# A router's 0/1 rows made by one comparison a token tile, and a transpose moved ahead of a score group

## Chip, cores and metric

One NeuronCore of a Trainium2 chip runs the whole program. The metric is device time in microseconds (us), the median of several runs. Engines are PE (matmul), DVE (vector), ACT (scalar), POOL (GpSimd), SP (issues DMAs).

## What is computed

Two transformer layers on 2048 tokens of width 512, each with a modulated layer norm, an attention and a feed-forward part.

```
x = x + ga * attn0(norm(x) * (1+ca) + sa)      # windows of 64, hop 32
x = x + gb * moe(norm(x) * (1+cb) + sb)        # 64 experts, 8 chosen per token
x = x + ga * attn1(norm(x) * (1+ca) + sa)      # window 128 and 16 first keys
x = x + gb * ffn(norm(x) * (1+cb) + sb)        # Hadamard, 512 -> 2048 -> 512
```

In `moe` each token goes to eight experts:

```
top_val, top_idx = lax.top_k(probs, 8)
mapping = jnp.where(replace, best_primary, jnp.arange(E))   # some experts merged into others
y = ragged_dot(silu(gate) * up, down)                       # rows sorted by expert
out = zeros.at[tok].add(y * w)
```

## The kernel before

The program is a row of blocks with a barrier of all engines between them: set-up, first attention with the router's scores, routing, experts, second attention, feed-forward. Inside a block every engine has a fixed program, and semaphores order them.

**Routing** turns the chosen experts into a table `slot_rows`: sorted by expert, the 16384 (token, expert) pairs fill up to SLOTS = 192 slot tiles of 128 places. A pair has a slot tile `part[:, 0]` (0 to 191) and a place in it `part[:, 1]` (0 to 127). The table with one token number a place is a sum of outer products on PE: for each of NT = 16 token tiles of 128 tokens, and each of TOPK = 8 choices j, a matmul (L995) of `hot_b` (128 tokens x 128 places, the token's number where the place is this pair's, else 0) by `hot_a` (128 tokens x 192 slot tiles, 1 or 0). All 128 add into bank 1. `hot_a` and `hot_b` are fp16, double buffered (GROUPS = 2): tile t waits until the matmuls of tile t - 2 are done (`table_mm`).

Each row of `hot_a` is one DVE instruction (L1083), so is each of `hot_b` for j below BY_DVE = 5 (L1085). For the other three ACT makes `|place - iota|` (L904) and then `relu(token - token * that)` (L907). PE waits for DVE (`hot_done`) and ACT (`hot_act`). Between the tables' matmuls PE does other work of the block: a Hadamard product of `wd` (L920, for token tiles 0 to 11) and a quarter of a modulation product (L928) a tile. ACT copies their results out (L883, L888, L890) in the same loop. Before the loop PE does two whole modulation products and two small transposes (L988), and DVE works out `part`. POOL has no work in this block. The block ends when DVE has written `slot_rows` (L1091) and ACT has copied the last modulation product.

**The second attention** works in turns written out by hand. In a turn tile s has its scores made, the tile before it, a, has its probabilities transposed and multiplied by the values, w gets the output projection, and y, p, f are later tiles being normalised and projected. PE's order in the last part of a turn is: the output projection of w (L1703), the transposes of a's fourth group of probabilities (`turn_probs(a, 3)`, L1645), the scores of s's fourth group (`scores(s, 3)`, L1635), two transposes of a's probabilities of the first 16 keys (L1715) and one of its inverted row sums (L1717, which raises `pM_mm`), the transposes of f's keys (L1724), and then the products that need what ACT copied: L1730 spreads the inverted row sums and waits for `pM_out`, raised by ACT's copies L1606 and L1607; L1733 and L1737 follow. ACT's order is the two copies of the fourth group (L1579), L1606, L1607, the copy of f's keys (L1617), the exponentials of s's fourth group (L1571). DVE's row maxima of s's fourth group (L1773) follow its scores and are DVE's last work of a turn.

Of the kernel before, what the change touches and what calls it, by code (L numbers as in the profile page):

```python
# [5 lines left out]
ALU = mybir.AluOpType  # L6
ACT = mybir.ActivationFunctionType
# [3 lines left out]
I32 = mybir.dt.int32  # L11
U32 = mybir.dt.uint32
F16 = mybir.dt.float16

P = 128
S, C = 2048, 512
NT = S // P
# [12 lines left out]
E = 64  # L30
TOPK, SELK = 8, 4
# [4 lines left out]
SLOTS = PAIRS // P + E  # L36
# [19 lines left out]
AHEAD = 3  # L56
# [54 lines left out]
def adaln_two_layers(nc, a, out):  # L111
    ctx = ExitStack()
    with ctx:
# [33 lines left out]
        route = sb("route", [P, 8 * C])  # L147
# [3 lines left out]
        slot_iota = sb("slot_iota", [P, SLOTS], F16)  # L151
# [645 lines left out]
        with ExitStack() as ph, nc.Block() as block:  # L797
# [2 lines left out]
            GROUPS = 2  # L800
            up_at, down_at = (lambda r: r * UPW), (lambda r: RING * UPW + r * DOWNW)
            cv = Carver(up_at(AHEAD))
            hot_a = cv(GROUPS * TOPK * SLOTS // 2).bitcast(F16).rearrange("p (b j n) -> p b j n", b=GROUPS, j=TOPK)
            assert cv.at <= RING * UPW
            cv = Carver(down_at(AHEAD))
            hot_b = cv(GROUPS * TOPK * P // 2).bitcast(F16).rearrange("p (b j n) -> p b j n", b=GROUPS, j=TOPK)
            assert cv.at <= KEPT
            cv = Carver(SCRATCH0)
            secT = cv(NT // 2 * P // 2).bitcast(BF16).rearrange("p (i n) -> p i n", n=P)
# [15 lines left out]
            slot_f = cv(NT, TOPK)  # L825
            slot_i = cv(NT, TOPK).bitcast(I32)
            part_i = cv(2, NT, TOPK).bitcast(I32)
            part = cv(2, NT, TOPK)
            minus, tok_minus = cv(NT, TOPK), cv(NT)
            BY_DVE = 5  # L830
            away = masked.rearrange("p t e -> p (t e)")[:, 0:GROUPS * (TOPK - BY_DVE) * P].rearrange("p (b j n) -> p b j n", b=GROUPS, n=P)
            cols, act_c = cv(KC), cv(KC)
            act_b = cv(KC, P)
            spare = cv(1)
# [4 lines left out]
                ("c_in", "rows_in", "ahead_in", "c_done", "c_wide", "cnt_mm", "secT_mm", "secT_out", "moves_done",  # L839
                 "chosen_mm", "chosen_done", "tot_mm", "rank_mm", "eid_done", "eid_mm", "hot_done", "table_mm",  # L840
                 "had_mm", "had_out", "mod_mm", "mod_out", "dve_steps"))
            parts_done, away_done, hot_act = (psem("r_" + n) for n in ("parts_done", "away_done", "hot_act"))
            wT_mm, wT_out, moves_wide, w_mm, w_out, w_stored = (
                psem("r_" + n) for n in ("wT_mm", "wT_out", "moves_wide", "w_mm", "w_out", "w_stored"))
            wm_in = [psem(f"r_wm_in{j}") for j in range(WMB)]
# [4 lines left out]
            @block.sync  # L850
            def _(sp):
                sp.dma_start(cols, a["c_cols"][:, 1]).then_inc(c_in, 16)
                for e in range(AHEAD):
                    sp.dma_start(arena[:, up_at(e):up_at(e) + UPW], a["moe_up"][e].rearrange("p k n -> p (k n)")).then_inc(ahead_in, 16)
                    sp.dma_start(arena[0:FH, down_at(e):down_at(e) + DOWNW], a["moe_down"][e].rearrange("p k n -> p (k n)")).then_inc(ahead_in, 16)
                w = a["L1_wmod"].rearrange("(k p) (j n) -> j p k n", p=P, j=6)
                sp.dma_start(routed.su_row, a["L1_ffn_SU_ug"].partition_broadcast(P)).then_inc(rows_in, 16)
                sp.dma_start(routed.down_row, a["L1_ffn_Wscale_dp"].partition_broadcast(P)).then_inc(rows_in, 16)
                sp.wait_ge(w_out, 2)
                sp.dma_start(h_moe[0:S, C:].rearrange("(t p) e -> p t e", p=P), routed.second.rearrange("p i (t e) -> p (i t) e", e=E)).then_inc(w_stored, 16)  # L860
                for j in range(WMB, 6):
                    sp.wait_ge(mod_mm, j - WMB + 1)
                    sp.dma_start(routed.wm[:, j - WMB], w[j]).then_inc(wm_in[j - WMB], 16)
                sp.wait_ge(w_stored, 16)
                sp.wait_ge(ahead_in, 32 * AHEAD)
                sp.wait_ge(rows_in, 32)

            @block.scalar
            def _(act):
                for n in range(2):  # L870
                    act.wait_ge(secT_mm, n + 1)
                    nc.scalar.copy(secT[:, 4 * n:4 * n + 4].rearrange("p i n -> p (i n)"), psum[6 + n][:]).then_inc(secT_out, 1)
                for n in range(2):
                    act.wait_ge(wT_mm, n + 1)
                    nc.scalar.copy(routed.secondT[:, 4 * n:4 * n + 4].rearrange("p i n -> p (i n)"), psum[2 + n][:]).then_inc(wT_out, 1)
                act.wait_ge(c_in, 16)
                nc.scalar.activation(act_c, cols, ACT.Silu).then_inc(c_done, 1)
                act.wait_ge(c_done, 1)
                nc.scalar.copy(act_b[:], act_c.unsqueeze(2).to_broadcast([P, KC, P])).then_inc(c_wide, 1)

                def had_copy(f):
                    act.wait_ge(had_mm, f + 1)
                    nc.scalar.copy(wd[:, f], had_bank(f)[:]).then_inc(had_out, 1)  # L883

                def mod_copy(j):
                    act.wait_ge(mod_mm, j + 1)
                    if j in (1, 4):
                        nc.scalar.add(mod[:, 1, j], mod_bank(j)[:], 1.0).then_inc(mod_out, 1)  # L888
                    else:
                        nc.scalar.copy(mod[:, 1, j], mod_bank(j)[:]).then_inc(mod_out, 1)  # L890
                for f in range(HAD0):
                    had_copy(f)
                for n in range(2):
                    act.wait_ge(w_mm, n + 1)
                    nc.scalar.copy(routed.second[:, 4 * n:4 * n + 4].rearrange("p i n -> p (i n)"), psum[6 + n][:]).then_inc(w_out, 1)
                mod_copy(0)
                mod_copy(1)
                act.wait_ge(parts_done, 1)
                for t in range(NT):
                    if t >= GROUPS:  # L900
                        act.wait_ge(table_mm, t - GROUPS + 1)
                        act.wait_ge(hot_act, t - GROUPS + 1)
                    for j in range(BY_DVE, TOPK):
                        nc.scalar.activation(away[:, t % GROUPS, j - BY_DVE], slot_iota[:, 0:P], ACT.Abs, bias=minus[:, t, j:j + 1]).then_inc(away_done, 1)  # L904
                    for j in range(BY_DVE, TOPK):
                        act.wait_ge(away_done, t * (TOPK - BY_DVE) + j - BY_DVE + 1)
                        last = nc.scalar.activation(hot_b[:, t % GROUPS, j], away[:, t % GROUPS, j - BY_DVE], ACT.Relu, bias=tok_f[:, t:t + 1], scale=tok_minus[:, t:t + 1])  # L907
                    last.then_inc(hot_act, 1)
                    if 1 <= t <= FT - HAD0:
                        had_copy(HAD0 + t - 1)  # L910
                    if t % KC == 1 and t > KC:
                        mod_copy(2 + t // KC - 1)
                mod_copy(5)

            @block.tensor
            def _(pe):
# [73 lines left out]

                for t in range(NT):
                    pe.wait_ge(hot_done, t + 1)
                    pe.wait_ge(hot_act, t + 1)
                    for j in range(TOPK):
                        mm = nc.tensor.matmul(psum[1][:, 0:SLOTS], hot_b[:, t % GROUPS, j], hot_a[:, t % GROUPS, j],  # L995
                                              start=(t == 0 and j == 0), stop=(t == NT - 1 and j == TOPK - 1))
                    mm.then_inc(table_mm, 1)
                    if HAD0 + t < FT:
                        had_product(HAD0 + t)
                    mod_part(2 + t // KC, t % KC)  # L1000

            @block.vector
            def _(dve):
# [67 lines left out]
                st.did(ts(part_i[:, 1], slot_i, P - 1, None, ALU.bitwise_and))  # L1071
                st.settle()
                step(nc.vector.tensor_copy(part, part_i))
                st.did(ts(minus, part[:, 1], -1.0, None, ALU.mult))
                st.did(ts(tok_minus, tok_f[:], -1.0, None, ALU.mult))
                st.settle()
                dve.sem_inc(parts_done, 1)
                st.did(ts(expert_end[:], tile_end[0:1], 1.0, None, ALU.add))
                for t in range(NT):
                    if t >= GROUPS:  # L1080
                        dve.wait_ge(table_mm, t - GROUPS + 1)
                    for j in range(TOPK):
                        last = ts(hot_a[:, t % GROUPS, j], slot_iota[:], part[:, 0, t, j:j + 1], None, ALU.is_equal)  # L1083
                        if j < BY_DVE:
                            last = ts(hot_b[:, t % GROUPS, j], slot_iota[:, 0:P], part[:, 1, t, j:j + 1], tok_f[:, t:t + 1], ALU.is_equal, ALU.mult)  # L1085
                    last.then_inc(hot_done, 1)
                dve.wait_ge(eid_mm, 1)
                st.did(nc.vector.tensor_copy(tile_expert[:, 0:SLOTS], psum[0][0:1, 2 * P:2 * P + SLOTS]))
                dve.wait_ge(table_mm, NT)
# [306 lines left out]
        with ExitStack() as ph, nc.Block() as block:  # L1396
# [230 lines left out]
            def _(pe):  # L1627
# [20 lines left out]
                def turn(y, p, f, s, a, w, z):  # L1648
# [55 lines left out]
                        mm.then_inc(wo_mm, 1)  # L1704
                    if a is not None:
                        turn_probs(a, 3)
                    if s is not None:
                        scores(s, 3)
                    if a is not None:
                        pe.wait_ge(meta_exp, a + 1)  # L1710
                        pe.wait_ge(kv_rows, p + 1 if p is not None else NT)
# [3 lines left out]
                            nc.tensor.transpose(bb[:, n * P:(n + 1) * P], prob_meta[:, a % 2, HM * n:HM * n + HM].rearrange("p h k -> p (h k)"), ident[:])  # L1715
                        pe.wait_ge(r_done, a + 1)
                        nc.tensor.transpose(bb[0:NHEAD, 2 * P:3 * P], rinv, ident[:]).then_inc(pM_mm, 1)  # L1717
                    if f is not None:
                        pe.wait_ge(kx_done, f + 1)
                        pe.wait_ge(q_in, f + 1)  # L1720
# [584 lines left out]
```

## Time and profile before

| | |
|---|---|
| time, median of 3 runs (lowest, highest) | 2185.28 us (2179.81, 2190.99) |
| the profiled execution: time, span | 2188.56 us, 2186.8 us |
| mean granted TensorE clock | 0.96 |
| busy share of the span: PE, DVE, ACT, POOL | 92%, 46%, 34%, 34% |

The span runs from the first to the last instruction. Routing lies from about 317 to 387 us, the second attention from about 1290 to 1620 us. A busy share is an average over the whole program; which engine bounds a stretch is read from that stretch.

### The profile page before, as it was taken

The numbers are of one execution on the slowest core, as the hardware profiler recorded it, in microseconds if no ns is written. First come the engines' busy times: TensorE is split into PE (matmuls) and PEld (weight loads), VectorE is DVE, ScalarE is ACT, GpSimd is POOL, SyncE is SP. The second block draws the span as 40 slices with busy tenths as digits, with TensorE's granted clock in tenths as the row PEclk, the third lists the DMA queues.
The fourth block names the chain that finished last, engine by engine and source line by source line (L and its number), as shares of the span: only waits on it lengthen the run. The fifth ranks groups of instructions, "written<-read, shape, count | busy, mean of one in ns | idle before, by whom it ended". The sixth has DMA issues, their size and how long they took to land. (4 is left out here: it accounts for less than half of the span.)

```text
span 2186.8 us, 38652 instructions
## 1 busy us (share of the span) xinstructions
PE 2005.2 (92%) x11187; PEld 1316.9 (60%) x11189; DVE 1000.3 (46%) x3238; ACT 742.6 (34%) x1747; POOL 732.9 (34%) x668
## 2 busy tenths in 40 slices
PE   4799868899999999999999479999889999999998
PEld 1666644455555555555555146656558878788787
DVE  2467659334455422222222267667644443443432
ACT  0233327222222222222222057777653332222222
POOL 1144320355555555445554355444401101011000
PEclk8799979999999999999999689999999999999999
DMA  6222522598877888888898211000011121121210
GB/s 239 99 78 80 185 82 90 138 225 203 201 182 187 199 192 198 218 218 195 199 240 193 81 33 32 25 15 4 30 33 65 58 82 63 58 77 67 77 68 20
DMA packets 107128, 258.55 MB, mean 118 GB/s; under 512 B 25488, under 2 KB 29200, under 8 KB 106896
## 3 DMA queue, kind: packets, MB, share of 16 engines
q1 hardware_dynamic: 68240, 163.61, 23.2%
q0 software_dynamic: 35552, 88.63, 20.0%
q10 hardware_dynamic: 3232, 4.95, 0.6%
q8 instruction: 63, 1.03, 0.2%
q14 instruction: 41, 0.34, 0.1%
HBM read 196.55 MB, written 59.54 MB: 117 GB/s over the span
## 5 line engine op out<-in xcount | busy, mean ns | idle before, releaser
L1241 PE MATMUL bank<-arena 128*128 x1272 | 440.1, 489 | 1.7 <-ACT arena L1282 0.9
L1194 POOL DMA_INDIRECT x_sum<-route,arena x158 | 254.4, 1610 | 187.4 <-DVE route L1358 157.6
L1241 PEld LDWEIGHTS bank<-arena 128*128 128x128 f32 x1272 | 230.1, 191 | 132.7 <-issue 7.0
L1258 PE MATMUL bank<-arena 96*128 x632 | 299.9, 597 | 2.9 <-issue 2.8
L1205 POOL DMA_INDIRECT arena<-h_moe,arena x158 | 156.1, 988 | 222.4 <-DVE arena L1352 211.8
L1345 DVE SCALAR_TENSOR_TENSOR arena<-arena,bank 128x192 f32<-128x192 f32 x159 | 66.0, 415 | 309.2 <-ACT arena L1277 308.6
L2010 PE MATMUL bank<-x_hi,w_hi 128*128 128x512 f32 x512 | 201.4, 393 | 6.0 <-DVE x_lo L2139 6.0
L2010 PE MATMUL bank<-x_lo,w_hi 128*128 128x512 f32 x512 | 203.2, 397 | 0.0
L2010 PE MATMUL bank<-x_hi,w_lo 128*128 128x512 f32 x512 | 202.1, 395 | 0.0
L1277 ACT ACTIVATE arena<-bank 128x192 f32<-128x192 f32 x159 | 52.8, 332 | 359.2 <-PE bank L1241 359.2
L1258 PEld LDWEIGHTS bank<-arena 96*128 96x128 f32 x632 | 107.4, 190 | 82.1 <-issue 81.8
L2214 DVE SCALAR_TENSOR_TENSOR ffn_arena<-bank,ffn_scales,mod 128x512 f32<-128x512 f32 x64 | 48.1, 752 | 227.4 <-PE bank L2010 178.7
L1272 ACT COPY arena<-bank 96x256 f32<-96x256 f32 x158 | 58.4, 369 | 224.8 <-PE bank L1232 224.8
L1571 ACT ACTIVATE arena<-arena 128x256 f32<-128x256 f32 x256 | 127.1, 503 | 13.9 <-DVE arena L1773 13.8
L1357 DVE COPY arena<-slot_rows 128x1 int32 (+1 forms) x158 | 24.3, 154 | 213.2 <-PE bank L1258 207.0
L1250 PEld LDWEIGHTS bank<-ident,arena 128*128 128x128 f32 x640 | 79.6, 141 | 64.2 <-issue 27.2
L1991 POOL TENSOR_TENSOR ffn_arena<-ffn_arena,neg_half 128x1 f32<-128x1 f32 x12 | 6.6, 551 | 330.3 <-DVE ffn_arena L2153 330.3
L2010 PEld LDWEIGHTS bank<-x_hi,w_hi 128*128 128x128 f32 x512 | 96.4, 188 | 31.6 <-issue 4.8
L2010 PEld LDWEIGHTS bank<-x_lo,w_hi 128*128 128x128 f32 x512 | 96.2, 188 | 21.4
L2010 PEld LDWEIGHTS bank<-x_hi,w_lo 128*128 128x128 f32 x512 | 96.1, 188 | 20.8
L1358 DVE TENSOR_TENSOR route<-bank,mod 128x512 f32<-128x512 f32 x158 | 107.6, 681 | 0.0
L1250 PE MATMUL bank<-ident,arena 128*128 128x128 f32 x640 | 96.9, 274 | 11.6 <-DMA arena<-h_moe,slot_rows 8.4
(345 smaller groups left out, 3503.8 us busy)
## 6 DMA issues: line engine op xcount, KB each, us to landing
arena<-in_moe_up SPq DMA_DIRECT2D x64, 768.0 KB, 6.2
ffn_arena<-in_ffn_up SPq DMA_DIRECT2D x61, 512.0 KB, 3.3
arena<-in_moe_down SPq DMA_DIRECT2D x64, 384.0 KB, 7.5
arena<-in_L_wmod SPq DMA_DIRECT2D x12, 1024.0 KB, 7.0
x_sum<-route SPq DMA_DIRECT2D x18, 256.0 KB, 2.8
x_res<-in_L_attn_x SPq DMA_DIRECT2D x1, 4096.0 KB, 17.6
h_moe<-arena SPq DMA_DIRECT2D x16, 256.0 KB, 2.1
x_sum<-x_res SPq DMA_DIRECT2D x16, 256.0 KB, 2.4
```

What stands on the lines that cost most here:

```text
L1194: nc.gpsimd.indirect_dma_start(out=x_sum[b], out_offset=bass.IndirectOffsetOnAxis(ap=st_dst[:, b], axis=0), in_=y[:, b], in_offset=None, c ...
L1205: nc.gpsimd.indirect_dma_start(out=xg[:, b], out_offset=None, in_=h_moe, in_offset=bass.IndirectOffsetOnAxis(ap=slots, axis=0)).then_inc(x ...
L1241: mm = nc.tensor.matmul(psum[2 + b][:, 0:2 * FI], xgT[:, b, k], up_ring[:, bass.ds((e % RING) * UPW + k * 2 * FI, 2 * FI)], start=(k == 0) ...
L1250: mm = nc.tensor.transpose(psum[b][:, k * P:(k + 1) * P], xg[:, b, k * P:(k + 1) * P], ident[:])
L1258: mm = nc.tensor.matmul(psum[6 + b][:], hiddenT[:, b, n], down_ring[:, bass.ds((e % RING) * DOWNW + n * C, C)], start=(n == 0), stop=(n == 1))
L1272: nc.scalar.copy(hiddenT[:, b], psum[4 + b][0:FH, 0:2 * P].rearrange("p (n q) -> p n q", n=2)).then_inc(hT_out, 1)
L1277: nc.scalar.activation(gate_act[:, b], psum[2 + b][:, 0:FI], ACT.Silu).then_inc(gate_done, 1)
L1345: nc.vector.scalar_tensor_tensor(hidden[:, b], gate_act[:, b], row_w[:, b:b + 1], psum[2 + b][:, FI:2 * FI], ALU.mult, ALU.mult).then_inc( ...
L1358: nc.vector.tensor_tensor(y[:, b], psum[6 + b][:], mod[:, 0, 5], ALU.mult).then_inc(y_out, 1)
L1571: nc.scalar.activation(some, some, ACT.Exp, bias=nmx[:, t % 2, n:n + 1], scale=-1.0, accum_out=esum[:, t % 2, n:n + 1]).then_inc(exp_done, 1)
L2010: mm = nc.tensor.matmul(bank, x, y, start=(n == 0), stop=(n == len(passes) - 1))
L2214: nc.vector.scalar_tensor_tensor(inner, up_bank[:], scales[:, 1, f:f + 1], gate_act[:, b], ALU.mult, ALU.mult).then_inc(inner_done, 1)
```

## The change

In routing the eight rows of a token tile are laid out with the choice j innermost, so that one tensor_tensor comparison (is_equal) makes all eight. Its first operand is a constant `places` (place number n repeated eight times, fp16), its second the tile's eight values of `part`, read again for each n. A tensor_scalar then multiplies `hot_b` by the token's number. ACT's part of the rows is gone. POOL makes `places` at the start of the block (an iota in int32 and a cast), in memory that `hot_a` uses later. PE reads each matrix with a step of eight elements. In the second attention `scores(s, 3)` moves behind the three transposes L1715 and L1717.

```diff
-            hot_a = ... .rearrange("p (b j n) -> p b j n", b=GROUPS, j=TOPK)
+            hot_a = ... .rearrange("p (b n j) -> p b n j", b=GROUPS, j=TOPK)
-            hot_b = ... .rearrange("p (b j n) -> p b j n", b=GROUPS, j=TOPK)
+            hot_b = ... .rearrange("p (b n j) -> p b n j", b=GROUPS, j=TOPK)
...
+            def _(pool):
+                st.did(nc.gpsimd.iota(places_i, [[1, SLOTS], [0, TOPK]], base=0, channel_multiplier=0))
+                st.settle()
+                nc.gpsimd.tensor_copy(places, places_i).then_inc(places_done, 1)
...
-                act.wait_ge(parts_done, 1)
                 for t in range(NT):
-                    (waits for table_mm and hot_act, three Abs, three Relu)
                     if 1 <= t <= FT - HAD0:
                         had_copy(HAD0 + t - 1)
...
                     pe.wait_ge(hot_done, t + 1)
-                    pe.wait_ge(hot_act, t + 1)
                     for j in range(TOPK):
-                        mm = nc.tensor.matmul(psum[1][:, 0:SLOTS], hot_b[:, t % GROUPS, j], hot_a[:, t % GROUPS, j],
+                        mm = nc.tensor.matmul(psum[1][:, 0:SLOTS], hot_b[:, t % GROUPS, :, j], hot_a[:, t % GROUPS, :, j],
...
-                st.did(ts(minus, part[:, 1], -1.0, None, ALU.mult))
-                st.did(ts(tok_minus, tok_f[:], -1.0, None, ALU.mult))
-                st.settle()
-                dve.sem_inc(parts_done, 1)
+                dve.wait_ge(places_done, 1)
                 for t in range(NT):
                     if t >= GROUPS:
                         dve.wait_ge(table_mm, t - GROUPS + 1)
-                    (13 tensor_scalar: hot_a for 8 j, hot_b for 5)
+                    st.did(tt(hot_b[:, g], places[:, 0:P], part[:, 1, t].unsqueeze(1).to_broadcast([P, P, TOPK]), ALU.is_equal))
+                    st.did(tt(hot_a[:, g], places, part[:, 0, t].unsqueeze(1).to_broadcast([P, SLOTS, TOPK]), ALU.is_equal))
+                    st.settle()
+                    ts(hot_b[:, g], hot_b[:, g], tok_f[:, t:t + 1], None, ALU.mult).then_inc(hot_done, 1)
...
                         turn_probs(a, 3)
-                    if s is not None:
-                        scores(s, 3)
                     if a is not None:
                         (waits; two transposes L1715, one L1717 -> pM_mm)
+                    if s is not None:
+                        scores(s, 3)
```

## Rows read from the trace of the kernel before

**Rows 1.** The page: busy time, share of the span, instructions of each engine.

```profile
PE 2005.2 (92%) x11187; PEld 1316.9 (60%) x11189; DVE 1000.3 (46%) x3238; ACT 742.6 (34%) x1747; POOL 732.9 (34%) x668
```

**Rows 2.** Windows: the table loop; us, busy us (instructions), granted clock, DMA share, GB/s.

```profile
346.50:385.50 39.00, 36.15 (x184) 19.35 (x184) 36.50 (x184) 37.59 (x105) 0.00 (x0) 1.00 0.13 46
```

**Rows 3.** Groups by form, 300 to 405 us: busy us, mean ns | idle, releaser.

```profile
L1083 DVE TENSOR_SCALAR arena<-slot_iota,arena 128x192 f16<-128x192 f16 x128 | 32.2, 292 | 3.3 <-PE bank L995 3.2
...
L1085 DVE TENSOR_SCALAR arena<-slot_iota,arena,tok_f 128x128 f16<-128x128 f16 x80 | 26.9, 336 | 0.0
...
L907 ACT ACTIVATE arena<-arena,tok_f 128x128 f16<-128x128 f32 x48 | 20.6, 516 | 0.0
...
L904 ACT ACTIVATE arena<-slot_iota,arena 128x128 f32<-128x128 f16 x48 | 16.3, 428 | 0.0
...
L995 PE MATMUL bank<-arena 128*128 128x192 f16 x128 | 13.1, 245 | 5.4 <-ACT arena L907 5.4
```

**Rows 4.** Timeline of routing: start us, us, engine, line, count, [idle, releaser].

```profile
338.92 0.18 DVE L1078 TENSOR_SCALAR expert_end<-arena 1x64 int32<-1x64 f32 x1
...
341.04 0.79 DVE L1083 TENSOR_SCALAR arena<-slot_iota,arena 128x192 f16<-128x192 f16 x4
...
343.61 0.38 PE L988 MATMUL bank<-ident,arena 128*1 128x128 f32 x2
...
346.58 0.82 PE L995 MATMUL bank<-arena 128*128 128x192 f16 x8 [2.58 <-ACT arena L907]
...
348.98 0.82 PE L995 MATMUL bank<-arena 128*128 128x192 f16 x8
...
349.64 1.05 PE L920 MATMUL bank<-wd,had 128*128 128x512 f32 x2
...
351.39 0.82 PE L995 MATMUL bank<-arena 128*128 128x192 f16 x8
...
384.24 0.82 PE L995 MATMUL bank<-arena 128*128 128x192 f16 x8 [0.32 <-ACT arena L907]
...
384.90 1.05 PE L928 MATMUL bank<-arena 128*128 128x512 f32 x2
```

**Rows 5.** Groups by form on DVE, whole span.

```profile
L702 DVE TENSOR_TENSOR route<-arena,iota_row 128x1024 bf16<-128x1024 f32 x8 | 9.8, 1225 | 0.3
...
L708 DVE TENSOR_TENSOR arena<-route 128x512 bf16<-128x512 bf16 x8 | 3.2, 405 | 0.0
...
L712 DVE TENSOR_TENSOR arena<-arena 128x128 bf16<-128x128 bf16 x16 | 2.9, 223 | 0.3
```

**Rows 6.** Groups by form on POOL, whole span.

```profile
L277 POOL IOTA arena<- 128x192 int32 x1 | 0.3, 283 | 0.0
...
L285 POOL CAST slot_iota<-arena 128x192 f16<-128x192 int32 x1 | 0.3, 342 | 0.0
```

**Rows 7.** Timeline of one turn of the second attention.

```profile
1447.29 1.04 PE L1645 MATMUL bank<-ident,arena 128*128 128x128 f32 x8
...
1447.92 1.07 ACT L1579 COPY arena<-bank 128x512 f32<-128x512 f32 x2 [0.66 <-PE bank L1645]
...
1448.25 0.74 PE L1635 MATMUL bank<-arena 32*128 32x272 f32 x8
...
1448.92 0.44 PE L1715 MATMUL bank<-ident,mod 128*128 128x128 f32 x2
...
1449.12 0.44 DVE L1773 CUSTOM_DVE_ANT_0 arena<-bank,mask 128x272 f32<-128x272 f32 x1 [0.94 <-PE bank L1635]
...
1449.31 0.60 PE L1724 MATMUL bank<-ident,arena 128*128 128x128 f32 x4
...
1449.67 0.36 ACT L1607 COPY arena<-bank 128x256 f32<-128x256 f32 x1
...
1450.17 1.12 PE L1730 MATMUL bank<-arena 16*128 16x128 f32 x8 [0.26 <-ACT arena L1607]
```

**Rows 8.** Group of L1730 in the second attention, 1290 to 1640 us.

```profile
L1730 PE MATMUL bank<-arena 16*128 16x128 f32 x128 | 18.9, 289 | 5.5 <-ACT arena L1607 5.5
```

More of the change, by code:

```diff
@@ L802, in adaln_two_layers @@
             cv = Carver(up_at(AHEAD))
-            hot_a = cv(GROUPS * TOPK * SLOTS // 2).bitcast(F16).rearrange("p (b j n) -> p b j n", b=GROUPS, j=TOPK)
+            hot_a = cv(GROUPS * TOPK * SLOTS // 2).bitcast(F16).rearrange("p (b n j) -> p b n j", b=GROUPS, j=TOPK)
             assert cv.at <= RING * UPW
             cv = Carver(down_at(AHEAD))
-            hot_b = cv(GROUPS * TOPK * P // 2).bitcast(F16).rearrange("p (b j n) -> p b j n", b=GROUPS, j=TOPK)
+            hot_b = cv(GROUPS * TOPK * P // 2).bitcast(F16).rearrange("p (b n j) -> p b n j", b=GROUPS, j=TOPK)
             assert cv.at <= KEPT
@@ L827, in adaln_two_layers @@
             part_i = cv(2, NT, TOPK).bitcast(I32)
[L828 to L831, printed above, removed]
+            part = cv(NT * TOPK).bitcast(F16).rearrange("p (a t j) -> p a t j", a=2, j=TOPK)
+            at = 2 * NT * E + TOPK * E + C + E
+            places = route[:, at:at + SLOTS * TOPK // 2].bitcast(F16).rearrange("p (n j) -> p n j", j=TOPK)
+            places_i = arena[:, up_at(AHEAD):up_at(AHEAD) + SLOTS * TOPK].bitcast(I32).rearrange("p (n j) -> p n j", j=TOPK)
             cols, act_c = cv(KC), cv(KC)
@@ L841, in adaln_two_layers @@
                  "had_mm", "had_out", "mod_mm", "mod_out", "dve_steps"))
-            parts_done, away_done, hot_act = (psem("r_" + n) for n in ("parts_done", "away_done", "hot_act"))
+            places_done, pool_steps = psem("r_places_done"), psem("r_pool_steps")
             wT_mm, wT_out, moves_wide, w_mm, w_out, w_stored = (
@@ L866, in _ @@
                 sp.wait_ge(rows_in, 32)
+            @block.gpsimd
+            def _(pool):
+                st = Steps(pool, pool_steps)
+                st.did(nc.gpsimd.iota(places_i, [[1, SLOTS], [0, TOPK]], base=0, channel_multiplier=0))
+                st.settle()
+                nc.gpsimd.tensor_copy(places, places_i).then_inc(places_done, 1)
             @block.scalar
@@ L897, in _ @@
                 mod_copy(1)
-                act.wait_ge(parts_done, 1)
                 for t in range(NT):
[L900 to L908, printed above, removed]
                     if 1 <= t <= FT - HAD0:
@@ L1081, in _ @@
                         dve.wait_ge(table_mm, t - GROUPS + 1)
[L1082 to L1086, printed above, removed]
+                    g = t % GROUPS
+                    st.did(tt(hot_b[:, g], places[:, 0:P], part[:, 1, t].unsqueeze(1).to_broadcast([P, P, TOPK]), ALU.is_equal))
+                    st.did(tt(hot_a[:, g], places, part[:, 0, t].unsqueeze(1).to_broadcast([P, SLOTS, TOPK]), ALU.is_equal))
+                    st.settle()
+                    ts(hot_b[:, g], hot_b[:, g], tok_f[:, t:t + 1], None, ALU.mult).then_inc(hot_done, 1)
                 dve.wait_ge(eid_mm, 1)
```

## The prediction, made before the changed kernel ran

> **What bounds the kernel now.** First the page: PE is busy 92% of the span [rows 1], so work taken from DVE or ACT is worth only what it frees PE from waiting for. The question for each half of the change is where PE waits today, and for whom. For routing I read the window of the table loop, then its groups, then its timeline. In the 39 us of the loop PE, DVE and ACT are all busy over 90% at full clock [rows 2]: three chains of nearly equal length. The groups give what PE waits for: before the tables' matmuls it idles 5.4 us, all put down to ACT's Relu, L907 [rows 3]. The timeline shows when: 2.58 us of it before the first table (PE is done with L988 at 343.99, the table begins at 346.58), and the tables then follow 2.41 us apart, at 348.98 and 351.39, with no wait of PE's between [rows 4]. So PE's own work makes the early period: 0.66 us from the table's first matmul to L920 [rows 4], that is 0.082 us a matmul, and 1.75 us for L920 and L928. The last table starts at 384.24; 15 periods after 346.58, (384.24 - 346.58) / 15 = 2.51 us on average. The four last tables have no L920 and still come at that pace: there ACT and DVE bound.
>
> For the second attention I read the timeline of one turn. PE has one gap: L1724 begins its four transposes at 1449.31 and ends at 1449.91, L1730 begins at 1450.17 after 0.26 us of idle, released by ACT's copy L1607 [rows 7]. Over the stage such gaps before L1730 sum to 5.5 us [rows 8].
>
> **Routing: DVE's new work.** Three instructions a tile take the place of 13: comparisons of 1024 and 1536 fp16 elements, and one scaling of 1024. No row shows an is_equal whose inputs are 16 bits. The nearest are: a tensor_tensor on bf16, 128 elements in 0.223 us and 512 in 0.405 (L712, L708), so 0.47 ns an element; and is_equal on fp32 inputs, 1024 elements in 1.225 us (L702) [rows 5]. By the first, 1024 elements take 0.223 + 896 x 0.47 ns = 0.65 us and 1536 take 0.89; by the second 1.23 and 1.84. I take the first, since the inputs' width is what the two have different and the change's are 16 bits with the innermost step 1. The Trainium skill (Vector Engine (DVE) Microarchitecture Reference, 5.1 Performance modes) says the same of such operands, a row that is read again included, and no row here shows it for a repeated one. For the scaling, four of L1083's come in 0.79 us, 0.17 apart for 192 elements [rows 4]; by the bf16 slope 1024 elements take at most 0.65, by half of it 0.4; I take 0.45. A tile is then 0.65 + 0.89 + 0.45 = 2.0 us with the short wait between comparison and scaling in it, and 3.5 (1.23 + 1.84 + 0.45) by the other end. DVE's rows now begin after L1078 at 338.92 [rows 4]; without `minus` and `tok_minus` a little earlier, about 338.6. Tile 0 is ready at 340.6 and tile 1 at 342.6, under PE's modulation products, so the 2.58 us go. POOL's iota and cast are eight times the 192 elements of 0.28 and 0.34 us [rows 6], at most 5.0 us from the block's start at 317, long before 338.6; if that cover failed it would be paid in full. SP's queue is passed by nothing. ACT loses L904 and L907, 16.3 + 20.6 us [rows 3], and keeps the copies that PE's banks wait for, which now come sooner.
>
> **Routing: PE with its reads as before.** Table 0 at 344.0; 12 tiles of 2.41 lead to 372.9 for table 12. DVE may run two tiles ahead, which 2.0 us a tile allows. Tiles 12 to 15 cost PE 0.66 + about 0.87, so DVE bounds: its tile 14 starts when table 12 is read (373.6) and is ready at 375.7 with the wait, and 15 at 377.8, where the last table begins. Before, 384.24: 6.4 us less.
>
> **Routing: PE with a step of eight.** This is the part that nothing in the trace prices: both matrices are now read with a step of 16 bytes, and before every operand of PE was contiguous in its innermost run. Below, nothing: 0.082 us for 192 columns is 0.43 ns a column. Above, I take the dearest column of the stretch: an fp32 product of 512 columns, two matmuls, takes the 1.75 us of L920 and L928 halved, 0.87 us, or 1.7 ns a column, four times as much. With a table's matmuls at twice the price (1.31 us a table) the last table's matmuls end at 344.0 + 12 x 3.06 + 3 x 2.18 + 1.31 = 388.6, against 384.90 before (the start of the last L928 [rows 4]): 3.7 us more. At four times (2.62 a table) they end at 344.0 + 12 x 4.37 + 3 x 3.49 + 2.62 = 409.5: 24.6 more. The change breaks even at about 1.08 us a table, 0.70 ns a column. I take no extra cost as the likeliest by a little, because in the fp32 products two bytes a column more cost no gap between matmuls that the profile shows; the doubt is large.
>
> The Trainium skill (SBUF — State Buffer, under "Door 1: The DMA port swizzle") speaks against it: SBUF has 16-byte lines, at least two accesses to a line are needed for full bandwidth, and each crossing to a new line costs a penalty. A step of exactly eight fp16 elements puts each column on a line of its own. It gives no figure; no row of before tells whether it holds for PE. By it the sum would be that of one of the two dearer cases.
>
> **Second attention.** PE's work stays the same, only its order differs. The transposes L1715 and L1717 begin at 1448.25 in place of 1448.92, so `pM_mm` comes 0.67 us sooner, at 1448.8. ACT's second copy L1579 ends at 1448.99 [rows 7]; L1606 and L1607 follow at once and end about 1449.5 in place of 1450.03. Then nothing holds L1730. Eight transposes, L1645, take 1448.25 - 1447.29 = 0.96 us, 0.12 each; L1724's four from 1449.31 would let L1730 begin at 1449.79: 0.38 us saved, or 0.26 by the gap alone. There are 15 gaps in the 5.5 us. In the last turn no scores are left to move, and the same order stays; I leave about 1.4 us there. So 4.1 us by the gaps, up to 5.8 if each of the 14 other turns gives the 0.12 more. I take 5.5, nearer the upper end, since PE's starts are what pace it. What moves later: s's fourth scores and DVE's maxima L1773, from 1449.12 to 1449.8. The first is there at 1450.2, and ACT, busy with L1607 until 1450.03 and then with the copy of f's keys (half of L1579's 1.07), takes the exponentials no later. The next turn's scores wait for the last maximum, four times 0.44 from 1449.8, at 1451.6; PE has L1730's 1.12 us and all of L1733 and L1737 before them. The waits of the moved transposes (`meta_exp`, `kv_rows`, `r_done`) are raised before the maxima of s's third group, which the fourth scores had to wait for anyway; so nothing is queued behind a new wait.
>
> **Sum.** 6.4 + 5.5 = 11.9 us off the profiled execution of 2188.56. The median of the runs is 3.3 us lower; the same off it gives 2185.28 - 11.9 = 2173.4 us. What this measurement can tell from no change is about 0.5%, or 10.9 us.
>
> **Rivals.**
> - *PE's strided reads at half speed:* +3.7 - 5.5, so 2183.5. For it: one column a line. Against: nothing in the trace.
> - *At a quarter, slower on the whole:* +24.6 - 5.5, so 2204.4. Place: the 128 matmuls L995; it makes the whole change slower from about 0.93 ns a column (5.5 us more over 16 tables than at break-even, 1.42 us a table). The row that speaks for it is only that fp32 columns cost that much, for their own reasons.
> - *The comparison isn't packed,* so one comparison is no saving: 3.5 us a tile on DVE, last rows ready at 338.6 + 56 = 394.6, the last L928 at 395.3: +10.4 - 5.5, so 2190.2. For it: the only is_equal row runs at the fp32 price.
> - *The wait in the attention only moves:* the exponentials come later and PE waits at the next `turn_probs`; routing alone, 2178.9.
>
> **Chances.** Forecast 0.42 (with it a measured gain over 0.5% at 0.65, since 11.9 lies just past 10.9); half speed 0.22; quarter 0.20; not packed 0.10; the wait moves 0.06. Faster by over 0.5%: 0.42 x 0.65 = 0.27. Slower: the quarter, 0.20, and a little of the unpacked case, 0.03. The rest, 0.50, is within. The range runs from 2168, the forecast with three us of scatter and the attention's upper end, to 2204, which takes in half speed, unpacked and half of the quarter case; what is left out is about 0.15. The forecast's own range is 2168 to 2179.
>
> **What would show it.** After: no ACT instructions between tables but copies; three DVE instructions a tile of 0.65, 0.9 and 0.45 us; L995's eight matmuls still 0.66 us from first to the next line, with the first table near 344.0 and the last near 378; L1730 without idle before it and 0.4 us less from L1645's start to L1730's than today's 2.88 [rows 7]. The prediction is wrong if a table takes over 1.1 us on PE, or a comparison over 1.2 us on DVE.

## The result and the profile after

| | before | after |
|---|---|---|
| median of 6 runs (lowest, highest) | 2184.67 us (2179.81, 2191.47) | 2208.53 us (2203.08, 2214.94) |
| span of the profiled execution | 2186.8 us | 2204.9 us |
| mean granted TensorE clock | 0.960 | 0.959 |

The ratio is 1.0109, 95% interval [1.0082, 1.0136]: 23.9 us slower by the medians, where 11.9 us less were forecast. The two profiled executions are only 18.1 us apart. Stages that the change doesn't touch scatter by some microseconds from one execution to the next (routing starts at 317.2 us in one and 321.4 in the other), so the stages are compared one by one below. Line numbers after are 4 lower for the table matmul (L995 is L991), 3 lower for the two products (L920 is L917, L928 is L925) and 7 lower for DVE's last lines of routing and in the second attention (L1717 is L1708, L1724 is L1717, L1730 is L1723).

The window of the table loop after, and groups by form from 300 to 430 us (busy us, mean ns, idle before), answer to [rows 2, 3]:

```profile
346.50:409.50 63.00, 63.00 (x172) 27.54 (x171) 28.15 (x42) 9.20 (x16) 0.00 (x0) 1.00 0.15 49
...
L991 PE MATMUL bank<-arena 128*128 128x192 f16 x128 | 46.7, 522 | 0.0
...
L991 PEld LDWEIGHTS bank<-arena 128*128 128x128 f16 x128 | 18.6, 146 | 26.8 <-issue 26.8
...
L1077 DVE TENSOR_TENSOR arena<-route,arena 128x1536 f16<-128x1536 f16 x16 | 15.2, 951 | 0.0
...
L1076 DVE TENSOR_TENSOR arena<-route,arena 128x1024 f16<-128x1024 f16 x16 | 11.1, 691 | 34.4 <-PE bank L991 34.4
...
L1079 DVE TENSOR_SCALAR arena<-arena,tok_f 128x1024 f16<-128x1024 f16 x16 | 7.8, 487 | 0.6
```

PE is busy for all of 63 us where [rows 2] had 36 of 39, DVE for 28. ACT has fallen from 37.6 to 9.2 us as told. A table matmul lasts 522 ns for the 245 of [rows 3], with the same shape. The three DVE instructions take 0.69, 0.95 and 0.49 us.

The timeline of routing after (start us, us) answers to [rows 4, 6]:

```profile
321.28 2.04 POOL L871 IOTA arena<- 128x1536 int32 x1 [11.58 <-POOLq L317]
...
323.39 1.46 POOL L873 CAST route<-arena 128x1536 f16<-128x1536 int32 x1
...
347.95 2.92 PE L991 MATMUL bank<-arena 128*128 128x192 f16 x8
...
350.69 1.04 PE L917 MATMUL bank<-wd,had 128*128 128x512 f32 x2
...
350.91 0.69 DVE L1076 TENSOR_TENSOR arena<-route,arena 128x1024 f16<-128x1024 f16 x1 [4.17 <-PE bank L991]
...
352.43 2.92 PE L991 MATMUL bank<-arena 128*128 128x192 f16 x8
...
412.50 2.92 PE L991 MATMUL bank<-arena 128*128 128x192 f16 x8
...
415.25 1.04 PE L925 MATMUL bank<-arena 128*128 128x512 f32 x2
```

POOL has made `places` at 324.9, long before DVE needs it. The first table follows the modulation products at once, at 347.95, and DVE's idle is now a wait for PE's matmuls. But L917 starts 2.74 us after the table does, against 0.66 in [rows 4], and the tables stand 4.48 us apart (347.95, 352.43) against 2.41. Eight matmuls in 2.74 us are 0.343 us each.

The timeline of one turn of the second attention after, and the group of its spread of the row sums, answer to [rows 7, 8]:

```profile
1445.33 1.04 PE L1638 MATMUL bank<-ident,arena 128*128 128x128 f32 x8
...
1445.97 1.07 ACT L1572 COPY arena<-bank 128x512 f32<-128x512 f32 x2 [0.66 <-PE bank L1638]
...
1446.20 0.38 PE L1706 MATMUL bank<-ident,mod 128*128 128x128 f32 x2
...
1446.62 0.74 PE L1628 MATMUL bank<-arena 32*128 32x272 f32 x8
...
1447.08 0.36 ACT L1600 COPY arena<-bank 128x256 f32<-128x256 f32 x1
...
1447.30 0.66 PE L1717 MATMUL bank<-ident,arena 128*128 128x128 f32 x4
...
1447.88 1.15 PE L1723 MATMUL bank<-arena 16*128 16x128 f32 x8
...
L1723 PE MATMUL bank<-arena 16*128 16x128 f32 x128 | 19.3, 292 | 1.6 <-ACT arena L1600 1.6
```

L1600, the copy that released L1730 before, is over at 1447.44, before the transposes of f's keys (L1717 after) end, and L1723 has no idle in front of it. The idle there fell from 5.5 to 1.6 us in all. From L1638's start to L1723's are 2.55 us, against 2.88 in [rows 7].

By stages, each from the trace's start times. Routing runs from its first DVE memset to the first DVE instruction of the next block, the attention from the first matmul that spreads row sums to the last of them:

| | routing block | 15 turns of the second attention |
|---|---|---|
| before | 317.2 to 387.6: 70.4 us | 1300.0 to 1613.6: 313.6 us |
| after | 321.4 to 417.9: 96.5 us | 1320.6 to 1631.3: 310.7 us |

So +26.1 and -2.9 us, 23.2 in all, and the medians say 23.9. The change is the sum of a large loss in one place and a small gain in another.

### The profile page after: what moved, and what is told of

It is laid out like the page before. It is cut to its first block and busy times, and to the rows that moved or that the text cites. A ratio compares the mean times of both kernels' runs of the same rounds, so it can differ in the third digit from the quotient of the medians.

```text
span 2204.9 us, 38367 instructions
## 1 busy us (share of the span) xinstructions
PE 2036.3 (92%) x11188; PEld 1328.4 (60%) x11189; DVE 997.4 (45%) x3076; ACT 710.3 (32%) x1651; POOL 735.6 (33%) x670
## 3 DMA queue, kind: packets, MB, share of 16 engines
q1 hardware_dynamic: 68240, 163.61, 23.2%
## 5 line engine op out<-in xcount | busy, mean ns | idle before, releaser
L1766 DVE CUSTOM_DVE_ANT_0 arena<-bank,mask 128x272 f32<-128x272 f32 x256 | 96.8, 434 | 21.9 <-PE bank L1628 21.9
```

The source lines that it names most:

```text
L1766: nc.vector.tensor_tensor_reduce(slot(t, c)[:, r], psum[r][:, 0:KEYS1], mask1[:, kind], -1.0, 3e38, ALU.add, ALU.min, accum_out=nmx[:, t % ...
```

## The experiments

### Step four, and the attention's part alone

The first question was which property of the new reads costs: that each column lies 16 bytes on, or that it isn't next to the last one. `step4` lays the eight choices out as two halves of four.

```diff
-hot_a = ... .rearrange("p (b n j) -> p b n j", b=GROUPS, j=TOPK)
+Q, H = 4, TOPK // 4
+hot_a = ... .rearrange("p (b h n q) -> p b h n q", b=GROUPS, h=H, q=Q)      # hot_b alike
-matmul(..., hot_b[:, t % GROUPS, :, j], hot_a[:, t % GROUPS, :, j], ...)
+matmul(..., hot_b[:, t % GROUPS, j // Q, :, j % Q], hot_a[:, t % GROUPS, j // Q, :, j % Q], ...)
```

> The changed kernel, with the eight choices laid out as two halves of four, so that PE reads both matrices with a step of four fp16 elements (8 bytes) in place of eight (16 bytes); DVE's three instructions a tile keep their element counts. If a column costs more only where it lies on a 16-byte line of its own, two columns share a line and a table's matmul comes every 0.08 to 0.12 us in place of 0.345; then the routing loop ends some 6 us sooner than in the kernel before, and with the attention's 4 to 5 us the time is about 2174 us, ratio 0.995. If any step over one costs (two fp16 elements read together when adjacent), the matmuls stay 0.345 us apart and the time is that of the changed kernel, about 2208 us, ratio 1.011. If the price follows the distance, about 0.17 to 0.2 us a matmul and about 2186 us.

Measured: ratio 1.001 [0.9997, 1.0022]. The timeline of its loop:

```profile
367.94 1.55 PE L992 MATMUL bank<-arena 128*128 128x192 f16 x8
...
369.32 1.04 PE L918 MATMUL bank<-wd,had 128*128 128x512 f32 x2
```

A table takes 369.32 - 367.94 = 1.38 us, 0.172 a matmul: half of step eight, twice step one. Two columns on one line did not bring back the old price, so the first theory is wrong as it was put. Between four and eight elements the price did follow the distance; step one had shown less than half of step four's. The routing block is 74.6 us, 4.2 more than before; with the attention's 2.9 less the stages give +1.3 us, which the interval holds.

`attn_only` is the kernel before with `scores(s, 3)` moved, nothing else.

```diff
                         turn_probs(a, 3)
-                    if s is not None:
-                        scores(s, 3)
                     ...two transposes L1715, one L1717...
+                    if s is not None:
+                        scores(s, 3)
```

> The kernel before with only the move of the fourth scores behind the three transposes. By the trace of the changed kernel a turn is 0.31 us shorter (20.95 for 21.27), so 4 to 5 us less in all: about 2180.5 us, ratio 0.998. The rival, that the wait comes back elsewhere in the turn or in the last turns: ratio 1.000.

Measured: 0.9995 [0.9983, 1.0006]. Its turns are those of the changed kernel (20.96 us; 310.8 for the 15), 2.8 us less than before, which the interval holds and can't tell from nothing. The expected 0.998 lies outside it: I had taken the 0.31 us for nearly every turn. The trace shows the gain, the timing alone doesn't.

### Which operand: the moving or the stationary one

Two kernels each give one matrix its old layout and leave the other. Each was run once; single runs scatter by some 15 us (17 of the kernel before lay between 2171.84 and 2186.72), so for single runs the stages of the trace are used. In the first pair DVE writes the contiguous rows with a step.

```diff
 # moving_only
-hot_b = ... .rearrange("p (b n j) -> p b n j", b=GROUPS, j=TOPK)
+hot_b = ... .rearrange("p (b j n) -> p b n j", b=GROUPS, j=TOPK)
 # stationary_only: the same edit on hot_a
```

> The changed kernel with hot_b's rows contiguous again (each j a run of 128 places), so that only the moving matrix hot_a has the step of eight. DVE writes hot_b with a step and should need 1.2 us or so for its comparison, still hidden. If the moving operand's reads set the pace, the matmuls stay 0.32 to 0.345 us apart; if the weight load does, they fall to 0.08 to 0.1. Time about 2206 us in the first case, about 2178 in the second.

> The changed kernel with hot_a's rows contiguous again, so that only the weights hot_b have the step of eight. DVE's comparison into hot_a is written with a step, about 1.8 us, and a tile of 3.0 us on DVE then bounds the loop at 16 x 3.0 = 48 us (about +4 us against the kernel before in routing). If the moving reads set the pace, a table's matmuls are 0.08 us apart, or about 0.15 if the load of strided weights (0.146 us mean in the changed kernel for 0.097) no longer hides; if the weights set it, they stay 0.345 apart.

Both were far slower, 2259.08 and 2257.87 us, for a reason of their own: DVE. `moving_only`, the granted clock in one window (last columns: clock, DMA share, GB/s), a table in the timeline, and DVE's groups:

```profile
361.40:364.00 2.60, 2.14 (x7) 0.87 (x8) 2.60 (x2) 0.00 (x0) 0.00 (x0) 0.50 0.00 0
...
361.86 2.88 PE L991 MATMUL bank<-arena 128*128 128x192 f16 x8 [1.58 <-DVE arena L1079]
...
364.56 1.89 PE L917 MATMUL bank<-wd,had 128*128 128x512 f32 x2
...
L1076 DVE TENSOR_TENSOR arena<-route,arena 128x1024 f16<-128x1024 f16 x16 | 78.7, 4917 | 0.0
...
L1079 DVE TENSOR_SCALAR arena<-arena,tok_f 128x1024 f16<-128x1024 f16 x16 | 40.1, 2506 | 0.6
```

The comparison written with a step of 128 elements takes 4.92 us for 1024 elements, where I expected 1.2. The table is still told well: 364.56 - 361.86 = 2.70 us, 0.338 a matmul, at a granted clock of 0.50, that is 1.2 GHz, after PE had idled for DVE. The changed kernel's 0.343 was at 1.00, 2.4 GHz. So this price doesn't depend on PE's clock. `stationary_only`, timeline:

```profile
372.31 1.50 PE L991 MATMUL bank<-arena 128*128 128x192 f16 x8 [3.09 <-DVE arena L1079]
...
372.77 7.01 DVE L1077 TENSOR_TENSOR arena<-route,arena 128x1536 f16<-128x1536 f16 x1
...
373.61 1.96 PE L917 MATMUL bank<-wd,had 128*128 128x512 f32 x2
```

Its table takes 373.61 - 372.31 = 1.30 us, 0.163 a matmul, at a granted clock of 0.50 too (its window from 372.31 to 373.60), and 192 columns at 1.2 GHz are 0.160 us: no extra cost of strided weights shows, but at this clock up to 0.16 could hide. Two of its sixteen tables ran at a granted clock of 1.00 (from 396.45 and 420.61): they took 0.73 and 0.71 us, about 0.09 a matmul, so little hides.

The second pair makes the contiguous rows by a comparison in that layout, written without a step, so that PE doesn't idle long and the clock stays up. The 1.75 us that one expectation takes from "the kernel with contiguous rows" is `rows_contiguous`, shown further on.

```diff
 # weights8: hot_a contiguous, hot_b with a step of eight; moving8 the other way round
-tt(hot_a[:, g], places, part[:, 0, t].unsqueeze(1).to_broadcast([P, SLOTS, TOPK]), is_equal)
+tt(hot_a[:, g], slot_iota[:].unsqueeze(1).to_broadcast([P, TOPK, SLOTS]), part[:, 0, t].unsqueeze(2).to_broadcast([P, TOPK, SLOTS]), is_equal)
```

> Only the moving hot_a keeps the step of eight; hot_b's rows are contiguous, made by an unpacked comparison (1.22 us). DVE takes 2.7 us a tile, below PE's 4.5. If the moving operand alone sets the price, 0.34 us a matmul at full clock, the same as at half clock in the earlier kernel, and a routing block as long as in the changed kernel, 96 us; if the price was that of both together, clearly less.

> Only the weights hot_b keep the step of eight; hot_a's rows are contiguous, made by a comparison that isn't packed (1.75 us, as in the kernel with contiguous rows) and written without a step, so that DVE takes 2.95 us a tile and PE's clock stays up. If only the moving operand pays per line, a matmul is 0.08 us apart, or up to 0.15 if the strided weight load (0.146 us for 0.097) is no longer hidden behind 192 columns. If weights pay per line as the moving operand does, 128 lines x 1.79 ns = 0.23 us a matmul, 1.8 us a table. Time about 2182 us in the first case.

`moving8`, timeline (one run, 2199.28 us):

```profile
362.88 2.88 PE L991 MATMUL bank<-arena 128*128 128x192 f16 x8
...
365.58 1.04 PE L917 MATMUL bank<-wd,had 128*128 128x512 f32 x2
```

`weights8`, timeline (one run, 2173.45 us, where 2182 was expected):

```profile
364.27 0.88 PE L991 MATMUL bank<-arena 128*128 128x192 f16 x8 [0.16 <-DVE arena L1079]
...
364.99 1.05 PE L917 MATMUL bank<-wd,had 128*128 128x512 f32 x2
```

2.70 us a table with only the moving matrix strided, as at half clock; 0.72 us, 0.090 a matmul, with only the weights strided. The moving operand sets the price. The weights add little: in `weights8` the first five tables took 0.66 us, as before, and the eleven after them, which start as soon as DVE has the rows ready, 0.72, or 0.008 us more a matmul. With a strided moving matrix they add the 0.005 between 0.343 and 0.338.

### Step two and step sixteen

`step2` is `step4` with Q = 2. `step16` interleaves the two buffers: `"p (n b j) -> p b n j"` for both matrices.

> As the kernel with a step of four, but four parts of two choices each, so that PE reads with a step of two fp16 elements (4 bytes). Prices of one table matmul of 192 columns so far: 0.082 us at step one, 0.172 at four, 0.345 at eight. If PE pays for each 16-byte line that the moving operand touches, 1.79 ns a line, 48 lines cost 0.086 us, hardly more than the columns themselves: about 0.09 a matmul, 0.7 a table, the routing block about 6 us shorter than before, with the attention's 2.9 the time about 2176 us, ratio 0.996. If any step over one costs the same until a line is left behind, 0.172 a matmul and ratio 1.001, as with four.

> The changed kernel with its two buffers interleaved, so that PE reads with a step of 16 fp16 elements (32 bytes); DVE's innermost run of eight stays. If lines touched set the price, it is that of step eight, 0.345 us a matmul, as every column has a line of its own in both. If the price follows the distance or the bytes spanned, 0.69 us a matmul, and the loop takes 44 us more than in the changed kernel.

`step2`, timeline: 

```profile
365.80 0.85 PE L992 MATMUL bank<-arena 128*128 128x192 f16 x8
...
366.49 1.05 PE L918 MATMUL bank<-wd,had 128*128 128x512 f32 x2
...
366.69 0.69 DVE L1078 TENSOR_TENSOR arena<-route,arena 128x1024 f16<-128x1024 f16 x1 [0.35 <-PE bank L992]
```

`step16`, timeline:

```profile
364.78 2.99 PE L991 MATMUL bank<-arena 128*128 128x192 f16 x8
...
367.60 1.04 PE L917 MATMUL bank<-wd,had 128*128 128x512 f32 x2
```

`step2`: a table in 0.69 us, 0.086 a matmul, DVE waiting for PE by a little. The ratio is 0.9953 [0.9933, 0.9972]: faster than both kernels. Its routing block is 64.2 us, 6.2 less than before. `step16`: 2.82 us, 0.352 a matmul; one run, 2218.76 us. The price rises with the step up to eight and then nearly stays. Both outcomes are those that the expectations worked out from lines touched, before these kernels ran; the other two, 0.172 for a step of two and 0.69 for sixteen, did not come.

### Contiguous rows by one comparison, and the halves alone

`rows_contiguous` makes both matrices as `weights8` makes hot_a.

> One comparison for eight rows, but in the layout of before (each j a contiguous row), so PE reads with step one and DVE reads each value of part again along the innermost axis. PE's matmuls go back to 0.082 us. If a comparison with an innermost step of zero on one operand is not packed, DVE takes about 1.2 and 1.75 us for the two, 3.5 us a tile with the scaling, and the routing block is about 10 us longer than before: about 2190 us. If it is packed, 2.0 us a tile, the block is 6 us shorter, about 2176 us.

Its two groups on DVE and one table:

```profile
L1077 DVE TENSOR_TENSOR arena<-slot_iota,arena 128x1536 f16<-128x1536 f16 x16 | 28.0, 1752 | 0.0
...
L1076 DVE TENSOR_TENSOR arena<-slot_iota,arena 128x1024 f16<-128x1024 f16 x16 | 19.5, 1218 | 0.0
...
363.23 0.83 PE L991 MATMUL bank<-arena 128*128 128x192 f16 x8 [0.74 <-DVE arena L1079]
```

One run: 2186.80 us; the routing block 78.0 us, 7.6 longer. A comparison is called packed here where it runs at about 0.65 ns an element and not at about 1.2. Without it DVE bounds and PE idles 0.74 us before a table. This is the third rival's case, and its price would have been 7.6 us, not 10.4: a tile takes 3.33 us on DVE (its comparisons start at 339.81, 343.14, 346.46), not 3.5, since the 1536 elements take 1.75 us for the 1.84 forecast and both comparisons start some 0.08 us before the instruction ahead of them has ended. Having a run of choices innermost is what makes the comparison packed (0.69 and 0.95 us in place of 1.22 and 1.75), and it is what makes PE's step.

`route_only` (the changed kernel with the old order of the scores) and `step2_old_order` (`step2` with it):

```diff
                         turn_probs(a, 3)
+                    if s is not None:
+                        scores(s, 3)
                     ...the three transposes...
-                    if s is not None:
-                        scores(s, 3)
```

> The changed kernel with the fourth scores back in their old place: routing's part alone. From the two traces the routing block is 26 us longer (96.5 for 70.4 us) and a turn of the second attention back at 21.27 us: about 2210 us. The rival, that the attention's change gains nothing or costs: the turns at 20.95 us or the time at or below 2207.

> The step of two in routing, with the fourth scores in their old place: routing's part of the faster kernel alone. By the traces the routing block is 6.2 us shorter than before and the second attention unchanged: ratio 0.997, about 2179 us. The kernel with both was 0.9953 [0.9933, 0.9972] where the two traces give 9.1 us, 0.9958. If the order of the scores were worth nothing, this kernel would be at 0.9953 too.

`route_only`, one run: 2214.56 us (about 2210 was expected), routing 96.6 us, turns 21.26 us. `step2_old_order`: 0.9979 [0.9962, 0.9997], routing 64.2 us, 15 turns 313.7 us (313.6 before); the expected 0.997 lies in the interval. The difference from 0.9953 is the attention's part, but the two intervals overlap, so its size is better read from the traces.

## Why the prediction failed

The routing figures of all kernels (the table's time is from its first matmul to the next product's, the median of 16 tables or one near it; steps in fp16 elements):

| kernel | step moving / weights | a table | a matmul | routing block |
|---|---|---|---|---|
| before | 1 / 1 | 0.66 us | 0.082 | 70.4 us |
| `step2` | 2 / 2 | 0.69 | 0.086 | 64.2 |
| `weights8` | 1 / 8 | 0.72 | 0.090 | 70.1 |
| `step4` | 4 / 4 | 1.38 | 0.172 | 74.6 |
| `moving8` | 8 / 1 | 2.70 | 0.338 | 95.9 |
| after | 8 / 8 | 2.74 | 0.343 | 96.5 |
| `step16` | 16 / 16 | 2.82 | 0.352 | 97.7 |

**The step that failed is "Routing: PE with a step of eight".** I took nothing of the two ends, 0.66 and 2.62 us a table; the truth was the upper end and a little over, 2.74. Put into the prediction's own sum it gives 344.0 + 12 x (2.74 + 1.75) + 3 x (2.74 + 0.87) + 2.74 = 411.5 for the last table's end, 26.6 us more than 384.90; the block grew by 26.1. The reason I gave for "nothing" was that fp32 operands, with more bytes a column, run without gaps. That was the wrong row for the question: those columns are adjacent, and the cost is one of columns that aren't. A reading that fits every row of the table is that the moving operand pays about 1.75 ns for each 16 bytes it reaches: 192 / 8 = 24 such pieces at step one hide behind the columns themselves (0.080 us at 2.4 GHz), 48 at step two (0.084 for 0.086 measured), 96 at step four (0.168 for 0.172), 192 at step eight (0.336 for 0.338), and 192 at step sixteen (0.336 for 0.352, a little above). Only three of the five points, steps four, eight and sixteen, lie clearly above what the columns themselves take, so the mechanism stays a reading: that the moving matrix's step sets the price is shown, why it does isn't. The reading was on record before `step2` and `step16` and both bore it out. All operands were fp16, so that the unit is 16 bytes and not eight elements is not shown. That the price is the same at half clock (0.338 at a granted 0.50) fits a wait that isn't in PE's own cycles.

The Trainium skill (SBUF — State Buffer, under "Door 1: The DMA port swizzle") names the same 16 bytes, and was named in the prediction as the rule that speaks against the change: rightly. But its finer part, that two accesses to a line are enough for full bandwidth, isn't what these runs show: at step four two columns share a line and a matmul costs 2.1 times as much; only at step two, four to a line, is it nearly free.

**The rival that came true is the quarter-speed one,** given 0.20 and 2204.4 us, with its place, the 128 matmuls, right. What it lacked is 4.1 us by the stages: 1.5 in routing (26.1 for 24.6) and 2.6 in the attention (2.9 for 5.5). The range's upper end, 2204, cut the rival off by half and missed the 2208.5. A rule that speaks against a change and a row that can't refute it should have had more weight than the lack of a row.

**What held in routing:** DVE's packed comparisons (0.69 and 0.95 us for 0.65 and 0.89; the scaling 0.49 for 0.45), as the bf16 rows said and as the Trainium skill has it (Vector Engine (DVE) Microarchitecture Reference, 5.1 Performance modes), which these runs bear out for a row read again (packed) and, in `rows_contiguous`, for one element read again (unpacked, 1.22 us). The change also made `part` fp16, where it was fp32, so that all operands of the comparison have 16 bits; no run kept it fp32. The wait for ACT before the first table is gone. POOL's part is hidden, 3.6 us for the 5.0 bound. `step2`, where PE's reads cost nearly nothing, gained 6.2 us for the 6.4 of the sum. So the rest of that sum was right, and one term of it wrong. The unpacked rival's 56 us for 16 tiles were 53 in `rows_contiguous` (16 x 3.33).

**The second attention: right mechanism, too large a size.** The term was 5.5 us; 15 turns took 2.9 less. L1730's wait is gone from all but the last two turns (1.6 us are left). The step that was mis-sized is the 0.38 us for each of 14 turns. From the fourth group's transposes to L1730 the starts stand 0.87, 0.22, 0.20, 0.68 and 0.58 us apart after, 2.55 in all, where the prediction kept the distances of before, 0.96, 0.28, 0.11, 0.67 and 0.48, or 2.50. Here a matmul's distance to the next changed with what came behind it. Each of the ten steady turns gives 21.27 - 20.96 = 0.31 us, 3.1 in all. The first gives 0.04, the last nothing, the two before the last 0.39 and 0.61. The turn in which DVE does the first extra row statistics got longer instead, 24.66 us for 23.41. PE idles 2.2 us there in both. Windows before, the idle and the work behind it:

```profile
1548.50:1550.70 2.20, 0.02 (x1) 0.00 (x0) 2.14 (x10) 1.07 (x5) 2.12 (x3) 1.00 0.51 145
...
1550.70:1555.70 5.00, 4.97 (x24) 2.72 (x25) 3.57 (x14) 4.04 (x15) 3.58 (x8) 1.00 0.63 251
```

And after:

```profile
1566.00:1568.10 2.10, 0.00 (x0) 0.00 (x0) 2.06 (x10) 1.03 (x5) 2.02 (x3) 1.00 0.52 152
...
1568.10:1574.70 6.60, 6.53 (x24) 3.90 (x25) 3.58 (x16) 4.19 (x15) 5.18 (x9) 0.74 0.48 190
```

Behind the same idle the granted clock stays at 1.00 before and falls to 0.74 on average after, that is to 1.2 GHz for part of it: 0.50 from 1568.1 to 1571.0. All ten kernels with the moved scores have this turn at 24.64 to 24.68 us; `before`, `route_only` and `step2_old_order` have it at 23.41. So 0.31 us were won in that turn and some 1.56 lost to the clock: the same work behind the idle took 5.04 us before (1550.73 to 1555.77) and 6.60 after (1568.17 to 1574.77). The fall isn't peculiar to the moved scores. One turn later PE idles 3.2 us in both kernels, and the clock falls behind it in both; before:

```profile
1569.90:1577.00 7.10, 7.10 (x28) 4.16 (x29) 3.83 (x13) 4.08 (x14) 6.23 (x5) 0.76 0.00 0
```

And after:

```profile
1588.50:1595.20 6.70, 6.64 (x25) 3.90 (x25) 3.38 (x13) 4.18 (x15) 5.74 (x5) 0.75 0.00 0
```

Over these two turns the kernel before pays for one fall and the changed one for two. Why the moved scores bring about the first is open: no run tried to fill the idle.

## What to carry to other kernels

A layout is paid for on both sides: making the innermost axis the one that lets DVE pack also sets the step at which PE reads, and the moving operand of every matmul pays for it. Look for the inner run that serves both: two elements kept DVE at its packed rate here and made PE's table matmuls 5% longer, and turned a loss of 1.1% into a gain of 0.5%. When the only price of an operation isn't in the trace, the row to ask is one with the same access pattern, and if there is none both ends have to be taken as likely.

## What was not expected of the hardware

- The price of a strided moving operand doesn't depend on the granted clock: 2.70 us a table at 0.50 and at full clock.
- DVE writing fp16 with a large step is very dear: 4.92 us for 1024 elements at a step of 128 elements (4.8 ns each) and 7.01 us for 1536 at a step of 192, against 1.22 and 1.75 us for the unpacked comparison that writes without a step. Which part of it is due to the step's size wasn't tried.
